# Eight layer norms of a decoder: halves made quarters, the mean folded into a centering product, the shift moved to ScalarE

## What is computed

```python
def _layernorm(x, axis=-1, eps=1e-05):
    m = jnp.mean(x, axis=axis, keepdims=True)
    v = jnp.var(x, axis=axis, keepdims=True)
    return (x - m) / jnp.sqrt(v + eps)

x = _layernorm(x + _L0_attn_ref(x, ...))                 # ln1, attention by distance, 16 heads
x = _layernorm(x + _L0_xattn_ref(x, ctx_1024, ctx_1024)) # ln2, an MLP whose weights are the 6404 context rows
x = _layernorm(x + _L0_ffn_ref(x, ...))                  # ln3, routed experts
x = _layernorm(x + _L1_attn_ref(x, ...))                 # ln4, attention with rotary positions
x = _layernorm(x + _L1_xattn_ref(ctx_1024, ctx_1024, x, mask, ...))  # ln5, attention over 6404 keys
x = _layernorm(x + _L1_ffn_ref(x, ...))                  # ln6
# inside _L1_ffn_ref:
#   x = x + _msa(_layernorm(x, ln1_w, ln1_b), w_qkv, w_proj)             lastn1
#   x = x + _moe_mlp(_layernorm(x, ln2_w, ln2_b), gate_w, gate_b, ...)   lastn2
```

## Time and profile before

| | |
|---|---|
| median of 3 runs | 2430.35 us (2428.01 to 2435.46) |
| the profiled execution's own time | 2432.52 us, of which the span of the trace is 2430.8 us |
| PE busy | 2217.4 us (91%) |
| PEld busy | 742.7 us (31%) |
| ACT busy | 1625.7 us (67%) |
| DVE busy | 961.2 us (40%) |
| POOL busy | 476.0 us (20%) |
| TensorE clock granted, mean | 0.958 of full |

### The profile page before, as it was taken

One profiled execution on the slowest core, in us unless ns is written; L12 is line 12 of the kernel. 1 busy time (PEld: TensorE's weight loads), 2 busy tenths in 40 slices (PEclk: granted clock), 3 DMA queues, 4 the chain that ended last, 5 costly groups with the idle time before them and its releaser, 6 DMA issues. The chain is left out here.

```text
span 2430.8 us, 30068 instructions
## 1 busy us (share of the span) xinstructions
PE 2217.4 (91%) x12022; PEld 742.7 (31%) x12022; DVE 961.2 (40%) x1480; ACT 1625.7 (67%) x1240; POOL 476.0 (20%) x254
## 2 busy tenths in 40 slices
PE   6899999689979988999899999999999977999897
PEld 2333333244436632222211111111111112222365
DVE  5766776325441156666211111110111115886112
ACT  1999989523333223555499999999999963666433
POOL 0577776201000024666300000000000000000000
PEclk9999999889989988999999999999999996999899
DMA  1000000046644002000100010010000000000010
GB/s 42 5 9 5 5 1 1 0 157 214 203 147 176 26 0 71 1 1 1 21 25 1 1 43 1 1 42 1 1 1 1 1 1 9 1 1 1 21 35 26
DMA packets 28989, 78.93 MB, mean 32 GB/s; under 512 B 3584, under 2 KB 18832, under 8 KB 26784
## 3 DMA queue, kind: packets, MB, share of 16 engines
q1 hardware_dynamic: 15032, 30.91, 4.2%
q0 software_dynamic: 4384, 29.56, 3.4%
q10 hardware_dynamic: 9448, 16.70, 1.9%
HBM read 71.62 MB, written 5.59 MB: 32 GB/s over the span
## 5 line engine op out<-in xcount | busy, mean ns | idle before, releaser
L1764 ACT ACTIVATE crat_E<-banks 128x1536 f32<-128x1536 f32 x544 | 749.4, 1461 | 20.7 <-PE banks L1664 6.9
L1680 PE MATMUL banks<-crat_E,crat_vst 128*32 128x512 f32 x3264 | 436.5, 607 | 0.2 <-ACT crat_E L1764 0.2
L1664 PE MATMUL banks<-crat_Q,mid_arena 52*128 52x512 bf16 x1632 | 328.9, 385 | 21.5 <-ACT crat_E L1764 17.3
L1791 DVE COPY crat_vst<-all_crossV 128x96 f32<-128x96 f32 x136 | 34.3, 253 | 640.6 <-PE banks L1680 640.5
L462 POOL TENSOR_TENSOR dist_wsum<-dist_wsum,dist_D 128x1024 f32<-128x1024 f32 x88 | 208.1, 2364 | 7.8
L1395 ACT ACTIVATE rotat_E<-banks 128x1024 f32<-128x1024 f32 x128 | 124.0, 1021 | 116.1 <-PE banks L1279 111.2
L344 DVE TENSOR_SCALAR dist_D<-banks,dist_k 128x512 f32<-128x512 f32 x256 | 178.5, 747 | 52.0 <-PE banks L217 52.0
L1664 PEld LDWEIGHTS banks<-crat_Q,mid_arena 52*128 52x128 bf16 x1632 | 60.2, 93 | 442.4 <-ACT crat_E L1764 316.8
L1461 DVE TENSOR_REDUCE rotat_mx<-banks 128x1 f32<-128x512 f32 x256 | 163.3, 686 | 69.6 <-PE banks L1250 68.4
L1395 ACT ACTIVATE lastat_E<-banks 128x1024 f32<-128x1024 f32 x128 | 123.9, 1020 | 85.2 <-PE banks L1271 85.2
L1461 DVE TENSOR_REDUCE lastat_mx<-banks 128x1 f32<-128x512 f32 x256 | 162.5, 685 | 37.2 <-PE banks L1250 34.5
(11 more groups left out here) (257 smaller groups left out, 2730.8 us busy)
## 6 DMA issues: line engine op xcount, KB each, us to landing
mlp_M<-in_mask POOLq DMA_DIRECT2D x28, 800.5 KB
mid_arena<-cross_k SPq DMA_DIRECT2D x42, 204.0 KB
moe_W<-in_experts SPq DMA_DIRECT2D x16, 512.0 KB, 3.6
mid_arena<-in_rot_tables ACTq DMA_DIRECT2D x8, 1024.0 KB, 18.5
mlp_C<-in_ctx SPq DMA_DIRECT2D x17, 384.0 KB, 4.5
cross_k<-mlp_kp ACTq DMA_DIRECT2D x17, 288.0 KB, 2.4
mlp_row<-in_mask POOLq DMA_DIRECT2D x1, 3202.0 KB, 12.8
mlp_M<-in_mask POOLq DMA_DIRECT2D x1, 3202.0 KB
```

The costliest lines, as they stand in the source:

```text
L1664: last = pe.matmul(PS[:, 3 * (at % 2) + k, :], K[s:s + ROWS, 2 * (g % 2) + pair, c * P:(c + 1) * P], Q[s:s + ROWS, 2 * g + pair, qh * HALF ...
L1680: last = pe.matmul(PS[32 * j:32 * j + 32, 6 + ps % 2, :], vst[:, (ps * STEPS + c // 3) % 3, c % 3, j, :], E[:, at // 3 % NE, at % 3, :], s ...
L1764: act.activation(flat(E[:, at % NE, :, :]), flat(PS[:, 3 * (at % 2):3 * (at % 2) + 3, :]), ACT.Exp, scale=CROSS_SCALE).then_inc(s_e, 1)
```

## The change

`layer_norm` works on four parts of 256 columns (`part(ap, k)`) in place of two halves of 512. There is a new constant `center`, the identity minus 1/128, loaded at the program's start by one more DMA of 64 KB (128x128 fp32), behind `ident` and ahead of `identb` and `cols`. The product of `z` with it is `z - mean` itself, in PSUM; the mean and the subtraction on DVE are no longer there, and `d` is not written to SBUF where there is no `scale`. ACT squares from PSUM, and DVE's last multiplication reads PSUM. The four centered parts take a bank each (`MID`), and the variances share two banks in turn (`VAR`), so that the third and fourth variance product wait for the Ln of the first and second.

ACT's order is now square 0, 1, 2, then Ln 0, Exp 0, square 3, and Ln, Exp of parts 1, 2 and 3; each Exp stands directly behind the Ln that it needs. PE's order is center 0, 1, 2, variance 0, center 3, variance 1, 2, 3. With `scale`, DVE does the multiplications by weight and by `r` in one instruction, and ACT adds the bias of each part with Identity, behind its last Exp. In lastn2 the sum `also` stands right behind the four additions.

The diff, without empty lines and, behind `layer_norm`, with one call of several alike:

```diff
@@ -472,11 +472,13 @@
                         total(p, 1)
-def layer_norm(nc, PS, name, onesd, resid, to, Y=None, bias=None, keep=None, also=None, scale=None, shift=None, early=None):
+def layer_norm(nc, PS, name, center, onesd, resid, to, Y=None, bias=None, keep=None, also=None, scale=None, shift=None, early=None):
+    PARTS = 4
+    W = T // PARTS
     with ExitStack() as ctx:
         n = Names(nc, ctx, name)
         z = keep if keep is not None else n.sb("z", [P, T])
@@ -484,11 +486,14 @@
         d = n.sb("d", [P, T])
         r = n.sb("r", [P, T])
         eps = n.sb("eps", [P, 1])
-        s_set, s_z, s_mean, s_d, s_sq, s_var, s_ln, s_r, s_m, s_out = (
-            n.sem(k) for k in ("set", "z", "mean", "d", "sq", "var", "ln", "r", "m", "out"))
+        s_set, s_z, s_d, s_sq, s_var, s_ln, s_r, s_m, s_out = (
+            n.sem(k) for k in ("set", "z", "d", "sq", "var", "ln", "r", "m", "out"))
         free = [b for b in range(8) if Y is None or b not in (Y, Y + 1)]
-        MEAN, VAR = free[0:2], free[2:4]
+        MID, VAR = free[0:PARTS], free[PARTS:PARTS + 2]
         src = z if Y is not None else resid
+        def part(ap, k):
+            return ap[:, k * W:(k + 1) * W]
         with nc.Block() as block:
             if early is not None:
@@ -499,54 +504,67 @@
             @block.vector
             def _(dve):
                 dve.memset(eps[:, :], LN_EPS).then_inc(s_set, 1)
-                for h in range(2):
+                for k in range(PARTS):
                     if Y is not None:
+                        of = PS[:, Y + k // 2, k % 2 * W:(k % 2 + 1) * W]
                         if bias is None:
-                            dve.tensor_tensor(half(z, h), PS[:, Y + h, :], half(resid, h), ALU.add).then_inc(s_z, 1)
+                            dve.tensor_tensor(part(z, k), of, part(resid, k), ALU.add).then_inc(s_z, 1)
                         else:
-                            dve.scalar_tensor_tensor(half(z, h), PS[:, Y + h, :], bias, half(resid, h), ALU.add, ALU.add
-                                                     ).then_inc(s_z, 1)
-                for h in range(2):
-                    dve.wait_ge(s_mean, h + 1)
-                    dve.tensor_tensor(half(d, h), half(src, h), PS[:, MEAN[h], :], ALU.subtract).then_inc(s_d, 1)
+                            dve.scalar_tensor_tensor(part(z, k), of, bias, part(resid, k), ALU.add, ALU.add).then_inc(s_z, 1)
                 if also is not None:
-                    dve.wait_ge(s_z, 2)
+                    dve.wait_ge(s_z, PARTS)
                     dve.tensor_tensor(also[0][:, :], src[:, :], also[1][:, :], ALU.add).then_inc(s_out, 1)
-                for h in range(2):
-                    dve.wait_ge(s_r, h + 1)
-                    dve.wait_ge(s_d, h + 1)
+                for k in range(PARTS):
+                    dve.wait_ge(s_r, k + 1)
                     if scale is None:
-                        dve.tensor_tensor(half(to, h), half(d, h), half(r, h), ALU.mult).then_inc(s_out, 1)
+                        dve.tensor_tensor(part(to, k), PS[:, MID[k], 0:W], part(r, k), ALU.mult).then_inc(s_out, 1)
                     else:
-                        dve.tensor_tensor(half(d, h), half(d, h), half(r, h), ALU.mult).then_inc(s_m, 1)
-                        dve.wait_ge(s_m, h + 1)
-                        dve.tensor_scalar(half(to, h), half(d, h), scale, shift, ALU.mult, ALU.add).then_inc(s_out, 1)
+                        dve.scalar_tensor_tensor(part(d, k), PS[:, MID[k], 0:W], scale, part(r, k), ALU.mult, ALU.mult
+                                                 ).then_inc(s_m, 1)
             @block.tensor
             def _(pe):
-                for h in range(2):
+                def variance(k):
+                    pe.wait_ge(s_sq, k + 1)
+                    if k >= 2:
+                        pe.wait_ge(s_ln, k - 1)
+                    pe.matmul(PS[:, VAR[k % 2], 0:W], onesd[:, :], part(sq, k), start=True, stop=True).then_inc(s_var, 1)
+                for k in range(PARTS):
                     if Y is not None:
-                        pe.wait_ge(s_z, h + 1)
-                    pe.matmul(PS[:, MEAN[h], :], onesd[:, :], half(src, h), start=True, stop=True).then_inc(s_mean, 1)
-                for h in range(2):
-                    pe.wait_ge(s_sq, h + 1)
-                    pe.matmul(PS[:, VAR[h], :], onesd[:, :], half(sq, h), start=True, stop=True).then_inc(s_var, 1)
+                        pe.wait_ge(s_z, k + 1)
+                    pe.matmul(PS[:, MID[k], 0:W], center[:, :], part(src, k), start=True, stop=True).then_inc(s_d, 1)
+                    if k >= 2:
+                        variance(k - 2)
+                variance(PARTS - 2)
+                variance(PARTS - 1)
             @block.scalar
             def _(act):
                 nc.scalar.preload_act_table_set("natural_log_exp_and_others")
-                for h in range(2):
-                    act.wait_ge(s_d, h + 1)
-                    act.activation(half(sq, h), half(d, h), ACT.Square).then_inc(s_sq, 1)
+                def inverse(k):
+                    act.wait_ge(s_var, k + 1)
+                    act.activation(part(r, k), PS[:, VAR[k % 2], 0:W], ACT.Ln, bias=eps[:, 0:1]).then_inc(s_ln, 1)
+                    act.wait_ge(s_ln, k + 1)
+                    act.activation(part(r, k), part(r, k), ACT.Exp, scale=-0.5).then_inc(s_r, 1)
                 act.wait_ge(s_set, 1)
-                for h in range(2):
-                    act.wait_ge(s_var, h + 1)
-                    act.activation(half(r, h), PS[:, VAR[h], :], ACT.Ln, bias=eps[:, 0:1]).then_inc(s_ln, 1)
-                for h in range(2):
-                    act.wait_ge(s_ln, h + 1)
-                    act.activation(half(r, h), half(r, h), ACT.Exp, scale=-0.5).then_inc(s_r, 1)
+                def square(k):
+                    act.wait_ge(s_d, k + 1)
+                    act.activation(part(sq, k), PS[:, MID[k], 0:W], ACT.Square).then_inc(s_sq, 1)
+                for k in range(PARTS):
+                    square(k)
+                    if k >= 2:
+                        inverse(k - 2)
+                inverse(PARTS - 2)
+                inverse(PARTS - 1)
+                if scale is not None:
+                    for k in range(PARTS):
+                        act.wait_ge(s_m, k + 1)
+                        act.activation(part(to, k), part(d, k), ACT.Identity, bias=shift).then_inc(s_out, 1)
 def context_mlp(nc, PS, x, w, Y, cross):
...
-def last_block(nc, PS, x, a, onesd, ident, identb, cols):
+def last_block(nc, PS, x, a, center, onesd, ident, identb, cols):
...
-            layer_norm(nc, PS, "lastn1", onesd, x, normed, scale=cols[:, 2:3], shift=cols[:, 3:4], early=operands)
+            layer_norm(nc, PS, "lastn1", center, onesd, x, normed, scale=cols[:, 2:3], shift=cols[:, 3:4], early=operands)
-        layer_norm(nc, PS, "lastn2", onesd, x, normed, Y=4, keep=xa, also=(xxa, x), scale=cols[:, 4:5], shift=cols[:, 5:6])
+        layer_norm(nc, PS, "lastn2", center, onesd, x, normed, Y=4, keep=xa, also=(xxa, x), scale=cols[:, 4:5], shift=cols[:, 5:6])
-        layer_norm(nc, PS, "ln6", onesd, xxa, x, Y=0)
+        layer_norm(nc, PS, "ln6", center, onesd, xxa, x, Y=0)
+        center = n.sb("center", [P, P])
...
+                sp.dma_start(center[:, :], a["center"]).then_inc(s_in, 16)
-                sp.wait_ge(s_in, 64)
+                sp.wait_ge(s_in, 80)
...
-        layer_norm(nc, PS, "ln1", onesd, x, x, Y=6, bias=cols[:, 0:1])
+        layer_norm(nc, PS, "ln1", center, onesd, x, x, Y=6, bias=cols[:, 0:1])
...
-        last_block(nc, PS, x, a, onesd, ident, identb, cols)
+        last_block(nc, PS, x, a, center, onesd, ident, identb, cols)
...
+        "center": (np.eye(P) - 1.0 / P).astype(np.float32),

```

More of the change, by code:

```diff
@@ L2134, in decoder @@
         context_mlp(nc, PS, x, a, 6, cross)
-        layer_norm(nc, PS, "ln2", onesd, x, x, Y=6)
+        layer_norm(nc, PS, "ln2", center, onesd, x, x, Y=6)
         with ExitStack() as mid:
@@ L2149, in decoder @@
                 routed_mlp(nc, PS, "moe0", x, ident, {"small": a["small0"], "experts": a["experts0"]}, ACT.Relu, True, early=pre)
[L2150 removed]
+                layer_norm(nc, PS, "ln3", center, onesd, x, x, Y=0)
                 operands = RotaryOperands(nc, inner, PS, x, pre, wide, K, Qb, Kb, V, wo, tiles)
```

5 lines of the change are left out of this document (2 added, 3 removed).

## The result

The changed kernel takes **2427.02 us** (median of 21 runs, 2424.63 to 2434.30); the kernel before, measured beside it, 2432.64 us (21 runs). The ratio is 0.9976, 95% interval 0.9968 to 0.9984, so 5.6 us were gained. The forecast had a gain of 9.5 us, a ratio of 0.9961, which lies outside the interval. Its time, 2420.9 us, was counted from a median of 2430.35 us for the kernel before; 2427.02 us is 6.1 more and lies near the upper end of the range, 2416 to 2428; 2.3 of the 6.1 are there because the kernel before, too, was measured slower this time.

What follows compares the result with a forecast made beforehand. The prediction took the eight norms, chains of waits between engines (75.75 us), as the piece to shorten. 10.0 us saved there less 0.5 at the start gave 9.5, so 2420.9 us from a median of 2430.35; range 2416 to 2428.

Steps and rivals of the forecast that it cites:

- The eight norms lose 10.0 us: All eight norm windows, walked instruction by instruction: savings of 1.0 to 1.5 us each, 10.0 us in sum.
- Start 0.5: Program start: the DMA of `center` ahead of `identb` and `cols` delays all engines, cost 0.5 us, between 0 and 1.
- Lastn1 and lastn2: The two norms with weight and bias: ends at 9.44 and 9.25 us, 1.13 and 1.37 less than before.
- the assumed low stretch: In ln3, TensorE at its lower clock level from 2.2 to 5.6 us, after the first mean product; 1.5 us less.
- what the chain loses or gains goes to the span whole: Norms: a block must end before the next stage begins, so the 10.0 us saved there shorten the span fully.
- a few us either way; that is in the range: Whole program: a shift of about a us can move any low-clock stretch of TensorE by a few us either way.
- rival (c): Stages behind the norms wait for something that does not move, so time stays at 2428 us or above; chance 0.08.
- Rival (a): Norms: ScalarE instructions don't overlap, four hand-overs a norm cost 0.17 us more each, time 2425.5 us; chance 0.2.
- Rival (b): Six stages behind norms lose 2.8 us each to TensorE's lower clock, 16.8 us, time 2447 us; chance 0.04.

Runs made afterwards that it cites:

- load_only: The kernel before with only the centering matrix loaded and not used: 2431.73 us, ratio 1.000 to the kernel before.
- two_fills: The changed kernel plus two products in TensorE's pause between lastn2 and ln6 and three behind ln4's last variance: 2421.55 us, ratio 0.9965 to the kernel before.

## Why the prediction was right in direction and too large

**"The eight norms lose 10.0 us": right, the closeness in part luck.** They lost 9.94. But ln3 came out 0.63 longer than walked and lastn1 0.52 shorter, both through the clock, and the two nearly cancel. In ln6 every price of the walk came out within 0.03: a part on ScalarE costs 0.81, Ln to Exp 0.50, a multiplication 0.42, the hand-over to it 0.03.

**"Start 0.5": mis-sized.** It was 0.05 in the first product (0.16 in `load_only`), and nothing that the time of `load_only` shows. The first product waits for another transfer.

**Lastn1 and lastn2: right sum, wrong picture.** The prediction put the last Identity behind VectorE's last instruction, with "the other three over by then". They stand behind the last Exp in ScalarE's order, so all four lie on the path: 1.59 us from the last Exp's end to the norm's, where the walk had 0.93. Lastn1 was still shorter than walked (8.92 for 9.44), as it ran at 0.81 instead of 0.66.

**ln3: the assumed low stretch was wrong.** It was taken as 2.2 to 5.6 us from the norm's start, as before, and fell differently: 8.13 for 7.5.

**The step that failed** is in the first paragraph: "what the chain loses or gains goes to the span whole". It goes into the start of the next stage, but the next stage isn't the same length. Between the norms 5.3 us were given back in one profile, 3.65 in the other. In the three stages shown, PE's busy time for the same instructions grew by 4.8 us, of 5.6 us that they became longer. The prediction had the price (a stage's beginning in 6.40 or 3.60 us) and then took the sign to be chance, "a few us either way; that is in the range". It had a sign where both profiles agree: behind ln1 +0.8, behind ln2 -1.0, behind ln4 +1.4 to +1.6, behind lastn2 +1.9. How far the cause is shown differs. At the end of the stage behind lastn2 it is shown: two more products in the pause, and nothing else, take 1.24 us off, and the same fill brings nothing in the kernel before. Behind ln4 it is shown that a low stretch at the stage's beginning costs this time, and that products at the end of ln4 remove it: twelve records in 7.08 us before, 8.36 after, 5.39 with the products (`two_fills`). That takes 3.4 us off where 1.6 were lost; it removes more than the change had added, so it isn't a pure return of the loss. 9.94 less 1.6 and 1.9 leaves 6.4; the stages behind ln1 and ln2 nearly cancel, and the stretch ahead of ln1 and the stage behind lastn1 differ from one execution to the next. So rival (c), "the gain is in the norms but not in the time", had the right heading, with "I find none" as its fault; it came true for some 4 of the 10 us, by another mechanism: in the rows shown the stages behind don't wait for something that did not move, their products run slower.

**Rival (a), ScalarE at full price, fell.** Spacing 0.81 in ln6, where (a) wanted 0.98. Its price of 0.17 a hand-over was too high by the prediction's own rows, too: Exp 0.40 and 0.03 behind it, less the 0.31 of the walk, is 0.12. The Trainium skill ("ScalarE: Activation LUTs", Rules for kernel authors) budgets about 0.3 us for an ACTIVATE and 0.83 ns for each element; that is an estimate of 0.51 for each instruction of 256 columns, 1.02 a pair, and the rows show 0.46 for Ln, 0.42 for Exp and 0.81 a pair. The same page, What ACT_TABLE_LOAD costs, states that back-to-back ACTIVATEs overlap by about 93 ns and that one with immediate scale and bias takes 186 ns beside its elements, each pointer operand about 93 more. With one overlap a pair, at the hand-over without a dependence, that is an estimate of 0.49 + 0.40 - 0.09 = 0.80; the trace agrees for the pair, though its Ln is 0.03 shorter and its Exp 0.02 longer.

**Rival (b), the clock,** had the right mechanism and too high a price: 2.8 us in each of six stages, 16.8 in all, where 3.65 to 5.3 were lost, 0.8 to 1.9 each in the three stages that lost in both profiles.

**Open.** What sets the place of a low stretch isn't settled. The old length with the new norm's instructions did not give the old stages; two kernels whose ln3 ran at the full clock had 5 us more behind it, and two others had not; the norm in halves had no loss behind ln4. The loss behind lastn1 was 2.0 us in one profile and 0.6 in the other, and it goes with the clock as well: the stage's first eight records take 5.33 us before, 6.55 and 5.50 after. Why they differ between two executions of one kernel no run shows. And the two fills' gain over the changed kernel (ratio 0.9965 against 0.9976) is plain in the two stages, but the intervals of the time overlap.

## What to carry to other kernels

Walk a chain of waits with the prices of its own rows: with spacings between instructions instead of durations, it was right to 0.01 us in the two norms that ran at the full clock; where the clock is low, the walk needs the place of the low stretch, and single norms were off by up to 0.6 us. Then ask, for every stage behind the piece that becomes shorter, at which clock its first and last products ran, since a pause of TensorE that was harmless may not stay so; two products in such a pause are a cheap test, in the kernel before as well as in the one after. And on an engine that works in order, put nothing behind the last instruction of the chain that another engine could do while it waits.
